# Routing of two experts of sixteen: the first pick taken from the shifted logits, the gates' products on another engine, and a new order

## The reference, cut to what matters

```python
s = softmax(u @ centroids.T + expert_biases)        # 16 experts
topk_vals, topk_idx = top_k(s, 2)                   # of equal values, the lower index first
g = sum(one_hot(topk_idx) * topk_vals[..., None])   # gates: s at the two picks, else 0
routed = sum_e g[e] * (u @ Wr[e].T + br[e])
return u + routed + shared(u)
```

## Time and profile before

| | |
|---|---|
| time before, median of 3 runs | 1730.34 us (1728.97 to 1731.37) |
| the profiled execution | 1738.31 us |
| its span, first to last instruction | 1736.3 us |
| granted TensorE clock, mean | 0.967 of full speed |
| busy | TensorE 1587.5 us, VectorE 1468.0, ScalarE 1019.6, GpSimd 906.0 |
| instructions | TensorE 12205, VectorE 3098, ScalarE 2110, GpSimd 1185 |
| chain that ended last | TensorE 53%, VectorE 34%, issue 5%, ScalarE 3%, others 5% |

### The profile page before, as it was taken

How to read it: one execution, slowest core, us unless ns; L and a number is a source line. 1 busy time by engine, 2 the same in 40 slices (tenths; PEclk the granted TensorE clock), 3 DMA queues, 4 the chain that set the end, 5 groups by cost and what they waited for, 6 DMA issues and landing times.

```text
span 1736.3 us, 33865 instructions
## 1 busy us (share of the span) xinstructions
PE 1587.5 (91%) x12205; PEld 1088.6 (63%) x12205; DVE 1468.0 (85%) x3098; ACT 1019.6 (59%) x2110; POOL 906.0 (52%) x1185
## 2 busy tenths in 40 slices
PE   3466899999999999999999999999999999999876
PEld 1334458576767767576767667576766767584735
DVE  5777989899998989899998989899998989883712
ACT  3343575757666574757666574757666575746262
POOL 6445364847456463837466464837455464732202
PEclk9788899999999999999999999999999999999897
DMA  4002020101102020101102020201102020201000
GB/s 110 1 7 55 8 56 8 50 15 31 39 8 62 2 63 7 55 15 31 40 11 59 2 62 8 58 13 31 38 8 62 2 63 2 59 5 52 12 14 6
DMA packets 66968, 53.34 MB, mean 31 GB/s; under 512 B 8370, under 2 KB 65522, under 8 KB 66802
## 3 DMA queue, kind: packets, MB, share of 16 engines
q1 hardware_dynamic: 65650, 50.41, 10.5%
q10 hardware_dynamic: 1152, 0.79, 0.1%
HBM read 8.44 MB, written 4.19 MB: 7 GB/s over the span
## 4 chain that ended last, share of the span: by engine, by line
PE 53%; DVE 34%; issue 5%; ACT 3%; SPq 2%; POOL 2%; DMA 1%; DVEq 0%; ACTq 0%; POOLq 0%
PE bank L952 49%; DVE rall L777 4%; PE bank L948 4%; DVE wkb L721 4%; DVE rall L775 4%; DVE rall L773 2%; DVE tree L682 2%; DVE inner L682 2%; DVE stats L673 2%; DVE ksum L708 2%; SPq L317 2%; DVE kvsum L713 1%; DVE kvb L701 1%; DVE mixed L682 1%; DVE tree L765 1%
## 5 line engine op out<-in xcount | busy, mean ns | idle before, releaser
L514 ACT ACTIVATE prob<-bank 128x512 f32<-128x512 f32 x640 | 356.1, 596 | 148.3 <-PE bank L952 146.6
L952 PEld LDWEIGHTS bank<-wexpT,prob 128*128 128x128 f32 x2048 | 263.4, 192 | 29.2 <-issue 24.9
L952 PE MATMUL bank<-kh,qh 72*128 72x512 bf16 (+3 forms) x1024 | 251.8, 305 | 30.2 <-DVE rall L775 14.1
L450 POOL TENSOR_TENSOR prob<-xdT,spread 128x512 f32<-128x512 f32 x128 | 163.1, 1274 | 221.3 <-ACT spread L514 192.1
L952 PE MATMUL bank<-wexpT,prob 128*128 128x128 f32 x2048 | 266.4, 276 | 0.0
L952 PE MATMUL bank<-qh,kh 75*128 75x512 bf16 (+3 forms) x1024 | 243.8, 303 | 8.6 <-ACT prob L514 6.0
L721 DVE RECIPROCAL wkb<-wkb 128x512 f32<-128x512 f32 x64 | 213.4, 3336 | 0.0
L514 ACT ACTIVATE spread<-bank 128x512 f32<-128x512 f32 x128 | 76.2, 596 | 224.7 <-PE bank L952 224.5
L777 DVE TENSOR_REDUCE rall<-bank 128x1 f32<-128x512 f32 x256 | 174.5, 682 | 24.2 <-PE bank L952 23.7
L952 PE MATMUL bank<-maskb,identb 128*128 128x128 bf16 x1024 | 192.9, 222 | 0.0
L952 PE MATMUL bank<-maskTb,identb 128*128 128x128 bf16 x1024 | 191.1, 220 | 0.0
(11 more groups left out here) (213 smaller groups left out, 3509.6 us busy)
## 6 DMA issues: line engine op xcount, KB each, us to landing
qh<-part SPq DMA_DIRECT2D x288, 64.0 KB
kh<-part SPq DMA_DIRECT2D x288, 64.0 KB
x<-in_L_attn_x_dram SPq DMA_DIRECT2D x16, 256.0 KB, 2.8
out_dram<-yo SPq DMA_DIRECT2D x16, 256.0 KB, 2.2
qh<-maxT SPq DMA_DIRECT2D x32, 24.0 KB
wk<-in_L_attn_tm_Wk_dram ACTq DMA_DIRECT2D x1, 256.0 KB, 5.7
wv<-in_L_attn_tm_Wv_dram ACTq DMA_DIRECT2D x1, 256.0 KB, 6.2
wr<-in_L_attn_tm_Wr_dram ACTq DMA_DIRECT2D x1, 256.0 KB, 6.4
```

The costliest lines, as they stand in the source:

```text
L450: raised(pool.tensor_tensor(ug[:, e % 4, :], xdT[:, :], spread[e // 2 % 2][:, :], ALU.mult), "ug_side")
L514: raised(act.activation(dst, src, func, **kw), signal)
L952: return pe.matmul(out_, w, x, start=start, stop=stop, **kw)
```

## The change

The first pick is made on the shifted logits: the largest logit is 0 there, so one instruction compares with 0 and multiplies by the rank. It needs neither the exponential nor the probabilities. The first pick is taken out by adding -3e38, and the second pick is made on what is left. The probabilities, the sum of the masks and the gates are computed by GpSimd (`gate_prob`, `gates`). Constants and counts that go with it: `TAKEN = -3e38`, `route` 6 to 5, `hot` gone, `gate_prob=2`; the tiles `eq1` and `m1` are gone.

```diff
@@ -439,6 +440,16 @@
                 until(pool, b, "gate_hi")
                 raised(pool.tensor_tensor(gate_rest[:, :, :], gts[:, :, :], gate_part[:, :, 0, :], ALU.subtract), "gate_rest")
 
+            def gate_probs(b):
+                until(pool, b, "route")
+                raised(pool.tensor_tensor(pe_[:, :, :], lex[:, :, :], wide(lin[:, :], NE), ALU.mult), "gate_prob")
+
+            def gates_of_both(b):
+                until(pool, b, "pick")
+                raised(pool.tensor_tensor(hots[:, :, :], hot1[:, :, :], hot2[:, :, :], ALU.add), "gate_prob")
+                until(pool, b, "gate_prob")
+                raised(pool.tensor_tensor(gts[:, :, :], pe_[:, :, :], hots[:, :, :], ALU.mult), "gates")
+
             def gate_low(b):
                 until(pool, b, "gate_mid")
                 raised(pool.tensor_tensor(gate_part[:, :, 2, :], gate_rest[:, :, :], gate_part[:, :, 1, :], ALU.subtract), "gate_lo")
@@ -464,7 +475,7 @@
                 **each("wk", C, weight_sum), **each("r_sig", C, receptance), **each("gated", C, gated), **each("rwkv", C, weighted),
                 "res": residual, "cmr_sig": channel_gate, "cmr_sum": channel_sum,
                 **each("rope_sum", 2, rope_sum), **each("rest", 2, first_rest), **each("part_lo", 2, third_part),
-                "gate_rest": gate_left, "gate_lo": gate_low, **each("u", SIDE, gated_input),
+                "gate_prob": gate_probs, "gates": gates_of_both, "gate_rest": gate_left, "gate_lo": gate_low, **each("u", SIDE, gated_input),
             }
             ones_of_heads(0)
             ones_of_heads(1)
@@ -816,35 +827,34 @@
                 raised(dve.tensor_reduce(lsu[:, :], lex[:, :, :], AX_X, ALU.add), "route")
                 until(dve, b, "route", 4)
                 raised(dve.reciprocal(lin[:, :], lsu[:, :]), "route")
-                until(dve, b, "route", 5)
-                raised(dve.tensor_tensor(pe_[:, :, :], lex[:, :, :], wide(lin[:, :], NE), ALU.mult), "route")
 
             ranks = rank[:, :].rearrange("p (o e) -> p o e", o=1).broadcast_to([P, J, NE])
 
-            def largest(b, second):
-
-                s, m, eq, key, km, hot = ((pe_, m1, eq1, key1, km1, hot1), (left, m2, eq2, key2, km2, hot2))[second]
-                done = 5 * second
-                until(dve, b, "pick", 5) if second else until(dve, b, "route")
-                raised(dve.tensor_reduce(m[:, :], s[:, :, :], AX_X, ALU.max), "pick")
-                until(dve, b, "pick", done + 1)
-                raised(dve.tensor_tensor(eq[:, :, :], s[:, :, :], wide(m[:, :], NE), ALU.is_equal), "pick")
-                until(dve, b, "pick", done + 2)
-                raised(dve.tensor_tensor(key[:, :, :], eq[:, :, :], ranks, ALU.mult), "pick")
-                until(dve, b, "pick", done + 3)
-                raised(dve.tensor_reduce(km[:, :], key[:, :, :], AX_X, ALU.max), "pick")
-                until(dve, b, "pick", done + 4)
-                raised(dve.tensor_tensor(hot[:, :, :], key[:, :, :], wide(km[:, :], NE), ALU.is_equal), "hot")
+            def largest_one(b):
+
+                until(dve, b, "route", 3)
+                raised(stt(key1[:, :, :], lsh[:, :, :], 0.0, ranks, ALU.is_equal, ALU.mult), "pick")
+                until(dve, b, "pick", 1)
+                raised(dve.tensor_reduce(km1[:, :], key1[:, :, :], AX_X, ALU.max), "pick")
+                until(dve, b, "pick", 2)
+                raised(dve.tensor_tensor(hot1[:, :, :], key1[:, :, :], wide(km1[:, :], NE), ALU.is_equal), "pick")
 
             def others(b):
-                until(dve, b, "hot", 1)
-                raised(stt(left[:, :, :], hot1[:, :, :], -2.0, pe_[:, :, :], ALU.mult, ALU.add), "pick")
-
-            def gates_of_both(b):
-                until(dve, b, "hot", 2)
-                raised(dve.tensor_tensor(hots[:, :, :], hot1[:, :, :], hot2[:, :, :], ALU.add), "hot")
-                until(dve, b, "hot", 3)
-                raised(dve.tensor_tensor(gts[:, :, :], pe_[:, :, :], hots[:, :, :], ALU.mult), "gates")
+                until(dve, b, "pick", 3)
+                raised(stt(left[:, :, :], hot1[:, :, :], TAKEN, lsh[:, :, :], ALU.mult, ALU.add), "pick")
+
+            def largest_two(b):
+
+                until(dve, b, "pick", 4)
+                raised(dve.tensor_reduce(m2[:, :], left[:, :, :], AX_X, ALU.max), "pick")
+                until(dve, b, "pick", 5)
+                raised(dve.tensor_tensor(eq2[:, :, :], left[:, :, :], wide(m2[:, :], NE), ALU.is_equal), "pick")
+                until(dve, b, "pick", 6)
+                raised(dve.tensor_tensor(key2[:, :, :], eq2[:, :, :], ranks, ALU.mult), "pick")
+                until(dve, b, "pick", 7)
+                raised(dve.tensor_reduce(km2[:, :], key2[:, :, :], AX_X, ALU.max), "pick")
+                until(dve, b, "pick", 8)
+                raised(dve.tensor_tensor(hot2[:, :, :], key2[:, :, :], wide(km2[:, :], NE), ALU.is_equal), "pick")
 
             def gated_input(b, e):
                 until(dve, b, "gb_ps", e + 1)
@@ -865,7 +875,7 @@
                 **each("tree", DEPTH, tree), "yb": add_tree, "moments4": lambda b: (until(dve, b, "yb"), moments(b, 4, yb)),
                 **each("rope_mul", 4, rope_product), **each("rowmax", UNITS, row_maxima), **each("max_join", 2, max_join),  **each("attend", 2, attended),
                 "yc": add_attention, "moments6": lambda b: (until(dve, b, "yc"), moments(b, 6, yc[b % 2])),
-                "route_logits": route_logits, "route_probs": route_probs, **each("largest", 2, largest), "others": others, "gates": gates_of_both,
+                "route_logits": route_logits, "route_probs": route_probs, "largest0": largest_one, "others": others, "largest1": largest_two,
                 **each("u", FRONT, gated_input), "yd": add_experts, "moments7": lambda b: (until(dve, b, "yd"), moments(b, 7, yd)),
             }
             def prepare_weights(b):
```

More of the change, by code:

```diff
@@ L34 @@
 MASKED = -1e30
+TAKEN = -3e38
 FREED_FOR_MAXIMA = 24
@@ L47 @@
     row_ps=UNITS, rowmax=UNITS, max_join=2, max_part=6, max_rest=4, maxT_ps=2, maxT=2, max_in=32, score_ps=UNITS, prob=UNITS, pv=16, pvT=2, back_ps=2, pv_inv=2, att=2,
-    attT_ps=1, attT=1, proj_ps=1, yc=1, xd=1, xdT_ps=1, xdT=1, logit_ps=1, route=6, lexp=1,
-    pick=9, hot=3, gates=1, gate_hi=1, gate_rest=1, gate_mid=1, gate_lo=1, gT_ps=1, gT=1, gb_ps=16, ug=8, spread_out=8, ug_side=8, expert_ps=16, yd=1, out_ready=1, stored=16,
+    attT_ps=1, attT=1, proj_ps=1, yc=1, xd=1, xdT_ps=1, xdT=1, logit_ps=1, route=5, lexp=1,
+    pick=9, gate_prob=2, gates=1, gate_hi=1, gate_rest=1, gate_mid=1, gate_lo=1, gT_ps=1, gT=1, gb_ps=16, ug=8, spread_out=8, ug_side=8, expert_ps=16, yd=1, out_ready=1, stored=16,
 )
@@ L56 @@
     pool="""
[L57 to L60, removed]
+        1:root1 4:gate_prob 4:gates 4:gate_rest 4:gate_lo 2:cmr_sig 2:cmr_sum 4:u1 4:u3 2:root3 3:max_left_hi0 4:u5 3:max_left_mid0 4:u7 4:u9 1:wk0
@@ L61 @@
+        4:u11 4:u13 4:u15 3:max_left_hi1 3:max_left_mid1 1:wk1 1:r_sig0 1:r_sig1 1:gated0 1:rwkv0 1:gated1 1:r_sig2 1:wk2 1:rwkv1 2:root_rms 1:wk3
+        1:gated2 1:r_sig3 2:rope_sum0 1:gated3 2:rest0 1:rwkv2 2:part_lo0 2:rope_sum1 1:rwkv3 2:rest1 2:part_lo1 0:root0 1:root2 0:x1_gain 0:x1_bias
+        2:root4 4:root7 3:root6 1:res
     """,
     act="""
-        4:route_exp 2:cmk_tanh3 2:cmr_tanh 1:norm1 3:norm4 4:gate_hi 4:gate_mid 4:gT_out 3:values 4:spread1 4:spread3 1:mix_before0 1:mix_before1
@@ L64 @@
[L64 to L67, removed]
@@ L79 @@
-        3:moments6 2:rowmax6 2:rowmax7 1:silu0 2:rowmax8 2:rowmax9 1:silu1 0:moments1 1:silu2 2:rowmax10 3:route_logits 2:rowmax11 3:route_probs
-        1:silu3 3:largest0 3:others 3:largest1 3:gates 2:rowmax12 2:rowmax13 2:rowmax14 2:rowmax15 2:rowmax16 3:u0
+        3:rowmax25 1:mix2 3:rowmax26 3:rowmax27 1:clamp0 4:u8 3:rowmax28 3:rowmax29 1:kv0 1:kvsum0 3:rowmax30 4:u10 2:tree0 3:rowmax31 1:ksum0
+        2:tree1 3:rowmax32 1:wkv0 3:rowmax33 3:rowmax34 4:u12 1:clamp1 2:tree2 3:rowmax35 2:tree3 3:rowmax36 3:rowmax37 4:u14 2:tree4 3:rowmax38
@@ new lines @@
+        3:score36 3:score37 1:read_out3 3:score38 3:score39 3:weigh12 3:weigh13 3:weigh14 3:weigh15 2:row0 2:row1 1:weights 3:back1 2:row2 2:row3
+        3:attT 1:xn2T 2:row4 2:row5 3:attn_out 2:attn_v 2:row6 2:row7 1:cmk0 1:cmk1 2:row8 2:row9 1:cmk2 2:row10 2:row11 3:xdT 1:cmk3 3:centroids
+        1:cmr 2:row12 3:shared 1:cmv0 1:cmv1 2:row13 1:cmv2 2:row14 2:row15 1:cmv3 3:gT 2:row16 2:row17 3:gb0 3:biases 2:row18 3:gb1 3:expert0 3:gb2
+        0:xnT 2:row19 2:row20 3:gb3 3:expert1 3:gb4 3:expert2 2:row21 2:row22 3:gb5 3:expert3 2:row23 2:row24 3:gb6
```

47 lines of the change are left out of this document (24 added, 23 removed).

## The result

After: 1711.63 us, median of 4 runs (1710.07 to 1714.23); before, beside them, 1730.03 us (1728.97 to 1731.37, 4 runs). The ratio is 0.9887, 95% interval 0.9870 to 0.9904. The forecast was 1717 us, 1705 to 1729, faster: the sign and the range held. The gain of the median was 18 us and not 14.

What follows compares the result with a forecast made beforehand. VectorE's routing ladder, then TensorE, held the chain. 14 routings x 0.70 = 9.8 us, 2.4 us for the last two and 2 us for order made 14 us off 1730.3: 1716, rounded up to 1717 us, range 1705 to 1729.

Steps and rivals of the forecast that it cites:

- The routing's step: Routing up to the first spread gate: starts at 752.27 in place of 752.97, gaining 0.70 us per full turn.
- the ladder: VectorE's chain of 19 small routing instructions per batch: five fewer, 1.3 us shorter up to row maximum 12.
- The gates on GpSimd: Sum and product moved to GpSimd: ready at 750.9, 0.3 us before TensorE asks, so no cost.
- ScalarE's exponential: Behind the last silu's tanh on ScalarE: ends at about 746.0, VectorE asks at 746.25, covered by 0.25 us.
- The term for the order: Rest of the new order: TensorE permuted without added work; VectorE's filled even-gate wait gives 0.3 us in seven turns, 2 us.
- The hits: VectorE tree instructions held by GpSimd products: mean taken as unchanged, 1.1 us each on VectorE; bounds -10.5 to +9 us.
- rival (a): Tree on VectorE: the new order removes all holds by GpSimd products, further 10.5 us, 1706 us; chance 0.18.
- the level-2 pair: Tree level 2 on VectorE beside GpSimd's odd expert product: 1.50 us in long turns, 0.38 in short; moved clear.
- near misses: Two pairs within 0.1 us of a GpSimd start: wkv0 beside weight sum 0, tree 5 beside the last odd product.
- Rival (b): VectorE late at the inverse each turn, so the gain is given back: 1726 us or no change; chance 0.18.
- Rival (c): One new hold of VectorE per turn, between even gates and first inverse: +4 us, 1735 us; chance 0.12.
- The wait for the heads: TensorE's 0.57 us wait at row 0 for the spread heads, hanging on SyncE's 18 issues: stays unchanged.

Runs made afterwards that it cites:

- the stretch alone: Kernel before with the new code and, of the new order, only the routing's stretch on VectorE, TensorE and ScalarE: 1720.02 us, ratio 0.9960.
- its complement: Changed kernel with the routing stretch of TensorE, VectorE and ScalarE put back in its old arrangement: 1717.94 us, ratio 0.9872.
- the turn's end: Moves of attend0, root 7, residual, weights' step: added to new code with only the routing stretch new, 1734.92 us; taken from the changed kernel, 1714.36 us.

## Why the prediction was right, and where it wasn't

**The routing's step held.** 0.70 us per full turn were predicted; the stretch alone gives 96.4 to 95.7, its complement loses 0.7. The single terms: the ladder 1.58 us shorter, not 1.3 (GpSimd's product at 738.96 held nothing, where 0.15 had been set aside, and the two independent rungs overlap by 0.11 and 0.17 us, not 0.1 each); transposition to spread gate as replayed (1.07 us). That half of the ladder's gain would be lost to TensorE's own products was right, and stronger than written: in the old order all of it is lost.

**The gates on GpSimd** were taken at nothing, covered by 0.3 us; the cover was 0.5 us. ScalarE's exponential came in time: `lex` 737.70 to 737.94, asked for at 738.46. In front of the odd gate's copy ScalarE is idle for 0.17 us and waits for its bank: the norm ahead of it isn't late.

**The term for the order is the one that was mis-sized.** The prediction says "The rest of the order permutes TensorE's work between 768 and 806 us without adding any", and gave the whole order 2 us, by the wait for an even gate in seven long turns. It is worth 0.4 us in every turn, 13 x 0.4 = 5 us. It isn't the turn's end, as two runs show. Against the kernel with the new stretch alone the first score starts 0.05 us earlier, the scores ahead of the read-outs 0.13, row 0 0.23, and the rows up to the channel mix gain 0.13 more; no single wait of TensorE's list differs. Which permutation does it stays open, since splitting the plan by engine broke it.

**The hits.** The sum took their mean as unchanged. The changed kernel has none in two profiled executions (its turns of 95.8 to 97.1 us are waits for transfers), nor have the five other kernels in which VectorE and GpSimd both have the new order: rival (a) was right in its mechanism, "the level-2 pair [...] is moved clear". The pair was not "the only one that tells long from short turns": level 5's does too, which is why a hit of 1.1 us had the price of 1.5 that the prediction took from the turns without saying where the rest came from. Of the near misses that I held against (a), one came true, on GpSimd's side (weight sum 0, 1.70 us), and a turn with less of it (1.41 us) is no shorter. The rival's size was wrong for the median: seven hits are how the one profiled execution fell, 1738.3 us; the runs shown were at 1729 to 1731 us. I had seen that 8 us difference and subtracted it, without asking whether it was the hits. It probably was for the most part: 7 x 1.6 = 11 us, less what hits the runs shown had. On the chip where the kernel before is at 1739 us the same order, but for the turn's end, brings 25 us, not 17.

**Put together**, for the 13 turns of the two profiled executions, where the hits can be counted: 13 x (0.7 + 0.4) + 7 x 1.6 = 25.5 us, where 25.0 were measured. For the medians: 13 x (0.7 + 0.4) + 2.1 = 16.4 us, less some 2.6 for the later start, leaves 4.6 of the 18.4 us measured, the price of about three hits. That last term is what is left over, not a count: unprofiled runs have no turns to count. So the 14 us predicted are near the 18 measured partly by luck: the order's term was 3 us too small and the hits' term, taken as nothing, some 4 to 5, while the later start took 2.6 back and the stretch behind the turns gave 1 less. A slip in the sum is small beside that: 5 x 0.255 + 0.2 less 0.2 is 1.3 us for each of the last two routings, not 1.2.

**Rival (b)**, the gain given back at the inverses, fell: the read-out starts 73.02 us behind the subtraction, not 73.99 as in a short turn before. **Rival (c)**, new hits in every turn, fell too for this change, but hits at new places did appear as soon as one engine's list was changed without the others. One sign named fell the other way: the mean turn is 1.9 us shorter, and more than 1.5 was to refute "the forecast as a whole". What it refutes is the terms for the order and the hits, not the routing's step. The wait for the heads stayed, as said: TensorE's matmuls wait for them in four turns before (3.5 us in all) and in four after (4.5 us). In the turn of the other rows it is its weight load that waits:

```profile
814.98 0.69 DVE L742 TENSOR_TENSOR x<-x,bank 128x512 f32<-128x512 f32 x1 [3.97 <-PE bank L962]
...
817.84 0.10 PEld L962 LDWEIGHTS bank<-kh,qh 72*128 72x128 bf16 x1 [0.41 <-DMA kh<-part]
```

At x2 VectorE now waits 3.97 us where it had waited 1.94. In the run with `attend0` back in front it is 1.5 there, and 1.2 ahead of `attend0`'s own division: as predicted, the move only says where VectorE's slack stands.

## What to carry to other kernels

Shortening a chain of small instructions on one engine pays only as far as the engine that waits for it has its own work arranged to be ready earlier; measure code and order apart, since here each was worth nothing or less alone and 17 us together. Lists of several engines written out by hand are one plan: moving one engine's half alone cost 5.4 us per turn. When a small instruction is held, follow the engine on from there: here the lateness that was left brought it beside the next product, and the second hit is some two thirds of what a long turn has more. When turns of one kernel have two lengths, count how many of each the profiled execution has before scaling a gain, and look at the spread of the plain runs: a race between two engines' starts had its bad outcome in one turn of 13 in one profiled execution and in twelve in another.
